# Mamba block with routed experts: the state's four output rows scaled on ScalarE and accumulated into y by DMA

## The reference

```
def step(s, inp):
    d_t, B_t, C_t, u_t = inp
    dA = jnp.exp(d_t[..., None] * A)
    dBu = d_t[..., None] * B_t[:, None, :] * u_t[..., None]
    s = s * dA + dBu
    y = jnp.einsum('bds,bs->bd', s, C_t)
    return (s, y)
...
y = y * jax.nn.silu(z)
```

## Time and profile before

| | us |
|---|---|
| median of 2 runs | 3052.15 |
| the profiled execution, as a run | 3054.61 |
| its span (first to last instruction) | 3052.8 |

### The profile page before, as it was taken

How to read it: one execution, slowest core, us unless ns; L and a number is a source line. 1 busy time by engine, 2 the same in 40 slices (tenths; PEclk the granted TensorE clock), 3 DMA queues, 4 the chain that set the end, 5 groups by cost and what they waited for, 6 DMA issues and landing times.

```text
span 3052.8 us, 52878 instructions
## 1 busy us (share of the span) xinstructions
PE 2488.1 (82%) x16524; PEld 1983.2 (65%) x16524; DVE 2568.1 (84%) x3986; ACT 1830.3 (60%) x3484; POOL 2563.1 (84%) x2379
## 2 busy tenths in 40 slices
PE   2566988879888797988879798887979888797979
PEld 0344766757676675767667576776757667576767
DVE  3579899888898988889898888889888898988953
ACT  2666666666666665665657566665656656665531
POOL 1689898989989898998989889898988989898942
PEclk7557998999999998999989899999989999999989
DMA  1311111211112111121112111121212211111101
GB/s 64 107 56 58 64 56 64 71 57 61 56 61 72 62 61 53 60 68 64 63 52 77 56 60 59 64 66 55 74 41 73 68 56 60 60 58 58 67 32 49
DMA packets 62150, 187.97 MB, mean 62 GB/s; under 512 B 12040, under 2 KB 14728, under 8 KB 61488
## 3 DMA queue, kind: packets, MB, share of 16 engines
q1 hardware_dynamic: 61872, 184.58, 18.0%
HBM read 166.68 MB, written 17.87 MB: 60 GB/s over the span
## 4 chain that ended last, share of the span: by engine, by line
POOL 29%; PE 27%; DVE 17%; issue 16%; ACT 9%; DVEq 1%; POOLq 1%; ACTq 0%; DMA 0%
POOL db_sb L639 12%; PE bank_ps L1236 9%; DVE states L995 7%; POOL y_sb L651 6%; PE moe_ps L1251 6%; PE rows_ps L1178 5%; POOL act L681 3%; POOL y_sb L659 2%; PE bank_ps L1160 2%; ACT da_ps L839 2%; DVE y_sb L1014 2%; DVE bank_ps L950 2%; DVE act L1089 1%; PE bank_ps L1134 1%; POOL du_sb L628 1%
## 5 line engine op out<-in xcount | busy, mean ns | idle before, releaser
L639 POOL TENSOR_TENSOR db_sb<-du_sb,b_sb 128x512 f32<-128x512 f32 x1024 | 1296.6, 1275 | 0.1
L1178 PE MATMUL rows_ps<-ident,states 128*128 128x128 f32 x4096 | 673.2, 295 | 163.7 <-DVE states L995 94.3
L651 POOL TENSOR_TENSOR y_sb<-y_sb,c_rows 128x512 f32<-128x512 f32 x512 | 655.1, 1280 | 169.8 <-ACT c_rows L817 169.8
L839 ACT ACTIVATE da_ps<-delta,a_sb 128x512 f32<-128x512 f32 x1024 | 701.8, 687 | 85.7 <-DVE states L995 84.2
L1178 PEld LDWEIGHTS rows_ps<-ident,states 128*128 128x128 f32 x4096 | 535.3, 153 | 281.9 <-DVE states L995 133.0
L1251 PE MATMUL moe_ps<-eout_sb,act 128*128 128x256 f32 x2304 | 627.7, 396 | 85.2 <-POOL act L681 83.5
L1236 PE MATMUL bank_ps<-h2T_high,ein_w_high 128*128 128x256 f16 x2304 | 644.0, 280 | 21.8 <-DVE delta L971 12.0
L995 DVE TENSOR_TENSOR_SCAN states<-da_ps,carry,db_sb 128x512 f32<-128x512 f32 x512 | 648.4, 1274 | 15.0 <-ACT da_ps L839 13.2
L1236 PE MATMUL bank_ps<-h2T_high,ein_w_low 128*128 128x256 f16 x2304 | 643.1, 279 | 0.0
L1236 PE MATMUL bank_ps<-h2T_low,ein_w_high 128*128 128x256 f16 x2304 | 642.4, 279 | 0.0
L995 DVE TENSOR_TENSOR_SCAN states<-da_ps,db_sb 128x512 f32<-128x512 f32 x512 | 616.2, 1213 | 23.2 <-ACT da_ps L839 13.0
(11 more groups left out here) (156 smaller groups left out, 2851.1 us busy)
## 6 DMA issues: line engine op xcount, KB each, us to landing
b_sb<-b_dram SPq DMA_DIRECT2D x128, 512.0 KB, 3.6
w_sb<-w_dram SPq DMA_DIRECT2D x128, 512.0 KB, 4.0
th_p<-x_dram SPq DMA_DIRECT2D x16, 512.0 KB, 5.8
r_dram<-conv SPq DMA_DIRECT2D x16, 512.0 KB, 2.6
x<-r_dram SPq DMA_DIRECT2D x16, 512.0 KB, 3.8
out_dram<-x SPq DMA_DIRECT2D x32, 256.0 KB, 2.2
mod_p<-mod_dram SPq DMA_DIRECT2D x8, 384.0 KB, 6.2
x<-e_in_dram SPq DMA_DIRECT2D x5, 512.0 KB, 4.6
```

The lines of the kernel that those rows point to most:

```text
L639: pool.tensor_tensor(db_sb[:, n % NDB, :], du_sb[:, slots[t][0][0], b, :], b_sb[:, k % NBPAIR, s % BPAIR, :], ALU.mult).then_inc(sem["scal ...
L651: pool.tensor_tensor(place, place, c_rows[:, n % NCR, :], ALU.add).then_inc(sem["c_added"], 1)
L839: ac.activation(da_ps[n % NDA][:, :], delta[:, slots[t][0][0], b, :], ACT.Exp, scale=a_sb[:, b, s:s + 1]).then_inc(sem["exp_done"], 1)
L1178: last = pe.transpose(rows_ps[j % 2][:, b * P:b * P + P], states[:, step % 2 * NB + b, j * P:j * P + P], ident[:, :])
```

## The change

All four groups of a state go the same way now. `c_scale` on ScalarE scales all four; two neighbouring groups (CPAIR = 2) go side by side into one buffer of c_rows, which has NCR = 3 buffers of 128x2x512. `c_add` no longer computes: for each pair GpSimd issues one accumulating DMA (512 KB) that adds c_rows to y_sb. It waits for the pair's second c_scale and for the same pair's transfer of the state before to have landed. `c_scale` waits for the transfer that last read its buffer. `y_gate` waits for the last transfer of its pair. `gather` is gone. To make room, db_sb has 5 buffers instead of 6 and w_sb holds 2 experts for each buffer instead of 4, so w_load runs twice as often with half the bytes. Some 20 due-time shifts change by fractions of a unit.

```
-NDA, NDB, NCR = 2, 6, 3
-C_ACT = (1, 3)
+NDA, NDB, NCR = 2, 5, 3
+CPAIR = 2
-WROWS, NWROWS = 4, 2
+WROWS, NWROWS = 2, 2
...
-            out += [(at + 0.145, ("c_scale", t, s, j)), (at + 0.892, ("c_add", t, s, j))] if j in C_ACT else [(at + 0.156, ("gather", t, s, j))]
+            out.append((at + 0.145, ("c_scale", t, s, j)))
+            if j % CPAIR == CPAIR - 1:
+                out.append((at + 0.892, ("c_add", t, s, j // CPAIR)))
...
-        c_rows = sb("c_rows", [P, NCR, DI])
+        c_rows = sb("c_rows", [P, NCR, CPAIR, DI])
...
+            def c_adds(n):
+                return sem[f"c_added{n % (NJ // CPAIR)}"], 16 * (n // (NJ // CPAIR) + 1)
...
-                    def c_add(t, s, j):
+                    def c_add(t, s, pair):
                         step = NS * nS(t) + s
-                        n = len(C_ACT) * step + C_ACT.index(j)
-                        pool.wait_ge(*c_scales(step, j))
-                        pool.wait_ge(sem["c_added"], max(0, n - len(C_ACT) + 1))
+                        n = NJ // CPAIR * step + pair
+                        pool.wait_ge(*c_scales(step, CPAIR * pair + CPAIR - 1))
+                        if step:
+                            pool.wait_ge(*c_adds(n - NJ // CPAIR))
...
-                        place = y_sb[:, slots[t][0][0], j, :]
-                        pool.tensor_tensor(place, place, c_rows[:, n % NCR, :], ALU.add).then_inc(sem["c_added"], 1)
+                        pool.dma_start(y_sb[:, slots[t][0][0], CPAIR * pair:CPAIR * pair + CPAIR, :], c_rows[:, n % NCR, :, :],
+                                       accum_op=ALU.add).then_inc(c_adds(n)[0], 16)
...
-                            pool.wait_ge(*((sem["c_added"], nS(t) * NS * len(C_ACT)) if j in C_ACT else (sem["gathered"], nS(t) * NS * len(C_DVE))))
+                            pool.wait_ge(*c_adds(NJ // CPAIR * (nS(t) * NS - 1) + j // CPAIR))
...
                     def c_scale(t, s, j):
...
-                        ac.wait_ge(sem["c_added"], max(0, n - NCR + 1))
-                        ac.activation(c_rows[:, n % NCR, :], rows_ps[j % 2][:, :], ACT.Copy,
+                        if n >= NCR:
+                            ac.wait_ge(*c_adds(n - NCR))
+                        ac.activation(c_rows[:, n % NCR, j % CPAIR, :], rows_ps[j % 2][:, :], ACT.Copy,
...
-                    def gather(t, s, j):
...
-                            pe.wait_ge(*(c_scales(*before) if before[1] in C_ACT else gathers(*before)))
+                            pe.wait_ge(*c_scales(*before))
```

More of the change, by code:

```diff
@@ L46 @@
 NPAIR = NE // 2 + 1
-NDA, NDB, NCR = 2, 6, 3
-C_ACT = (1, 3)
-C_DVE = tuple(j for j in range(NJ) if j not in C_ACT)
+NDA, NDB, NCR = 2, 5, 3
+CPAIR = 2
 NBANK = 3
@@ L140 @@
 TICK, ROUTED, UNITS_END = 1.4601, 16.0, 63.872
-SOFT = 45.462
+SOFT = 45.427
 Z_AHEAD, Y_SOON, Y_LATE = -0.26, -2.597, 0.993
 SLOT = 67.197
[L144 to L152, removed]
@@ new lines @@
+SHIFT = {"b_load": 0.39, "b_store": 0.49, "c_add": 0.79, "c_scale": 0.59, "delta": -0.77, "dt_bias": 0.09, "du": -0.32, "e_act": -0.12,
+         "e_mul": -0.12, "e_tanh": -0.35, "e_weigh": 0.65, "ein_load": 0.17, "ein_low": 0.44, "eout_fold": 0.63, "eout_load": -0.11,
+         "exp": 0.87, "expert_in": -0.12, "expert_out": 0.65, "gather": 0.59, "h2_high": 0.21, "h2_low": 1.04, "h_rms": -0.31,
+         "h_scale": -0.62, "h_square": -0.36, "hn_high": -0.93, "hn_low": -0.62, "hn_t": -0.65, "logit_exp": 0.21, "op": 0.69,
+         "op_gate": 0.69, "out_add": -0.12, "out_gate": -0.21, "out_store": 0.38, "r_add": 3.69, "r_gate": -0.15, "r_store": 0.35,
+         "router": 1.67, "rows": 0.41, "scaled": -0.1, "scan": -0.15, "skip": -1.61, "skip_evac": -0.34, "skip_t": -0.32, "soft_exp": -0.4,
+         "soft_ln": 0.93, "tap": 0.14, "u": -0.55, "u_tanh": -0.55, "w_evac": 0.99, "w_load": -0.12, "w_t": 0.94, "x1": 0.69,
+         "x1_norm": 0.93, "x1_rstd": -0.41, "x1_stat": 0.69, "x_load": -2.41, "x_rstd": -0.61, "x_scale": 0.42, "x_stat": 0.15,
+         "xd_t": -0.08, "xd_t_evac": 0.27, "y_evac": 0.39, "y_gate": -0.15, "y_t": 0.69, "z": -0.44, "z_gate": -0.51, "z_tanh": -0.45}
@@ L306, in adaln_block @@
                 "e_tanhed", "e_acted", "e_weighed", "expert_out_done", "out_gated", "out_added",
-                "exp_done", "scaled_done", "c_scaled", "c_added", "scan_done", "carried", "rows_full", "gathered",
+                "exp_done", "scaled_done", "c_scaled", "c_added0", "c_added1", "scan_done", "carried", "rows_full",
                 *(f"bank_{what}{n}" for what in ("full", "free") for n in range(NBANK)),
@@ L466, in h_done @@
                 return bank_read(("x_norm", t, half))
-            def gathers(step, j):
-                return sem["gathered"], len(C_DVE) * step + C_DVE.index(j) + 1
             def c_scales(step, j):
-                return sem["c_scaled"], len(C_ACT) * step + C_ACT.index(j) + 1
+                return sem["c_scaled"], NJ * step + j + 1
+            def c_adds(n):
+                return sem[f"c_added{n % (NJ // CPAIR)}"], 16 * (n // (NJ // CPAIR) + 1)
             def walk(steps):
@@ L813, in c_scale @@
                         step = NS * nS(t) + s
-                        n = len(C_ACT) * step + C_ACT.index(j)
+                        n = NJ // CPAIR * step + j // CPAIR
                         ac.wait_ge(sem["rows_full"], NJ * step + j + 1)
-                        ac.wait_ge(sem["c_added"], max(0, n - NCR + 1))
-                        ac.activation(c_rows[:, n % NCR, :], rows_ps[j % 2][:, :], ACT.Copy,
+                        if n >= NCR:
+                            ac.wait_ge(*c_adds(n - NCR))
+                        ac.activation(c_rows[:, n % NCR, j % CPAIR, :], rows_ps[j % 2][:, :], ACT.Copy,
                                       scale=xd_sb[:, slots[t][0][0], j, AT_C + s:AT_C + s + 1]).then_inc(sem["c_scaled"], 1)
@@ L1001, in carries @@
                         return sum(max(0, min(NS, step + 1 - NS * nS(t))) for t in halves)
-                    def gather(t, s, j):
-                        step = NS * nS(t) + s
-                        par = slots[t][0][0]
-                        v.wait_ge(sem["rows_full"], NJ * step + j + 1)
-                        if step:
-                            v.wait_ge(*gathers(step - 1, j))
-                        if s == 0 and t > 0 and slots[t - 1][1] is not None:
-                            v.wait_ge(*bank_read(("skip_t", t - 1, NB - 1)))
-                        place = y_sb[:, par, j, :]
-                        v.scalar_tensor_tensor(place, rows_ps[j % 2][:, :], xd_sb[:, par, j, AT_C + s:AT_C + s + 1], place,
-                                               ALU.mult, ALU.add).then_inc(sem["gathered"], 1)
                     def z_gate(t, j):
@@ L1115, in _ @@
                     walk({"ein_low": ein_low, "x_stat": x_stat, "x_scale": x_scale, "x_shift": x_shift, "tap": tap,
-                          "u": u, "xd_evac": xd_evac, "delta": delta_, "hn_low": hn_low, "h2_low": h2_low, "scan": scan, "gather": gather,
+                          "u": u, "xd_evac": xd_evac, "delta": delta_, "hn_low": hn_low, "h2_low": h2_low, "scan": scan,
                           "z_gate": z_gate, "op_gate": op_gate, "x1": x1_, "x1_stat": x1_stat, "router": router, "e_act": e_act, "e_mul": e_mul,
```

## The result

The changed kernel takes 3092.01 us, the median of two runs (3088.16 and 3095.86), against 3052.15 before: 1.28% slower, ratio 1.0128, 95% interval 1.0096 to 1.0160. That is within 2%, so the two kernels count as about equal; but the whole interval lies above 1, while 2930 us, a gain, was forecast.

What follows compares the result with a forecast made beforehand. GpSimd was taken as the bound: 120.5 us kept plus 33.3 of issues plus 18 idle make a slot of 171.8 us instead of 179.4. Over sixteen slots that is 122 us off 3052, so 2930 us, full range 2800 to 3250.

Steps and rivals of the forecast that it cites:

- The bound: Whole slot of 179.4 us: GpSimd, 160.0 us busy and 19.4 idle, sets the pace.
- The price of an issue: GpSimd's 32 DMA issues a slot: 1.04 us each, 33.3 us, bounded by 0.32 and 2.37 us.
- The idle time: GpSimd's waits in a slot: 18 us, of which c_rows 9, y_gate's landing 3, w_sb 2.5, expert product 1.5.
- the prediction's formula: Slot length as GpSimd's busy plus idle time: 138.5 + 32 p us, p the price of an issue, with 18 us idle.
- The landing: At the slot's turn, y_gate waits for the last transfer: lands after about 5.5 us, GpSimd stands 3 us.
- Costed at nothing: Five db_sb buffers, 128 more issues on SyncE's queue and three c_rows buffers: no time added.
- The wait at the head of ScalarE's list: ScalarE's c_scale waits delay exps and scans: taken as nothing, another 10 us a slot if VectorE's room were gone.
- Rival (a): GpSimd's issue is dear: slower from 1.40 us an issue, 3217 us at 1.6; 22 in 100.
- Rival (b): DMA engines become the bound: accumulating transfer at four times a copy's time, 6.2 us, gives 3868 us; 8 in 100.
- Rival (c): GpSimd's issue costs only 0.32 us, TensorE takes over: slot 165.4 us, time 2828 us; 12 in 100.
- Rival (d): Nothing to be seen, about 3040 us; sign: scans wait for exps 8 us a slot or more; 20 in 100.
- The inner range: Forecast's own range, 2850 to 3010 us: issue price from 0.8 to 1.16 us, idle time 3 us off either way.

Runs made afterwards that it cites:

- the kernel without additions: Kernel before the change with GpSimd's 512 additions of c_rows to y_sb left out, all else as it was: 2968.6 us, ratio 0.9718.
- the one with half the transfers: Kernel before with only GpSimd's additions (groups 1 and 3) replaced by one accumulating transfer a state: 3080.3 us; with the last state on GpSimd 3028.5 us.

## Why the prediction was wrong, point by point

- **The bound.** This step failed: "GpSimd is thus the main bound and the sum below goes by its time". Time freed on GpSimd arrives by 5.1 in 39.5, as the kernel without additions shows. In the middle GpSimd, TensorE and VectorE are all near full; at the turn nearly the whole price of the transfers is paid (11.8 of 12.7 us). Adding busy and idle time of one engine treats its idle time as a sum of waits that can be costed one by one, but idle time is where the other engines' pace shows.
- **The price of an issue.** 1.04 us was taken. Measured by GpSimd's busy time it is (149.9 - 120.5) / 32 = 0.92 us, 846 ns for one after idle. The busy-like time of 153.8 us was nearly right (149.9). But the additions were counted by the pitch, and by the pitch an issue is 0.61 us; the rest is lateness. That 1.04 us came near is luck: the row it was taken from is an operation on 4 elements. The Trainium skill ("DMA: Bandwidth & Descriptors", "Specifications") has about 1 us to a first byte on this path; no view here shows a first byte, and the smallest copy has landed 1.8 us after its issue began.
- **The idle time.** This is the term of the sum that was mis-sized: 18 us were forecast, 31.8 came: c_rows 14.6 instead of 9 (177.0 / 12.11), w_sb 3.4 instead of 2.5, delta 2.8 instead of 1, the same pair's earlier transfer 2.2 instead of 0, the norms' steps 3.2 where about 1 was taken for all short steps. It turned 7.6 us of gain into 2.3 of loss. By the prediction's formula with the measured 0.92 the slot would be 167.9 us; it is 181.7.
- **The landing.** Right in size: 5.8 us to land (about 5.5 forecast), 3.4 us of y_gate's wait (3 forecast). Wrong in weight: it was one term among GpSimd's waits, but TensorE stands behind it too, with the steps of the turn behind it. Keeping the last landing away from y_gate gave 30 us in the changed kernel and 52 in the one with half the transfers.
- **Costed at nothing.** The three c_rows buffers and the same pair's earlier transfer: ScalarE waits 20.9 / 12.11 = 1.7 us a slot for a buffer and GpSimd 2.2 for the pair. The wait at the head of ScalarE's list: "I take nothing", but c_scale behind a stand of 8.8 us holds TensorE and GpSimd in state 3.
- **Left out.** What 512 KB transfers at a DMA share of 0.69 do to others: x lands after 8.2 us instead of 5.8, and VectorE waits 2.8 us a slot for it.
- **The due-time shifts.** Not costed at all. They cost 31 us, where the loss against the kernel before is 40. They do not explain the miss: without them the kernel stands at 3060.8 us, not at 2930.
- **Rival (a)**, a dear issue: price below its threshold of 1.28, so not this. **Rival (b)**, the DMA engines as the bound: 2.80 us a transfer against a forecast of 3.1, a DMA share of 0.69 against some 0.74, so they fit, as was said. But an engine share under 1 was not free: 72 us come with the accumulation's size. The Trainium skill ("Collectives: The Full Stack", "The bandwidth ceiling") has a reduction among cores at half a copy's rate for its two source reads; the traces agree with the ratio, 2.15 times the copy's time, and show nothing of its cause. **Rival (c)**: not reached. **Rival (d)**, "nothing to be seen", was nearest, at 3040 us, and partly by the way it named, head-of-line waits on ScalarE. Its sign came short of its 8 us: scans waited 87.6 / 12.11 = 7.2 us a slot for exps, and VectorE had 40 us of idle time for that.
- The inner range of 2850 to 3010 us does not follow from its own terms. At p = 0.8 the formula gives 164.1 us, less than rival (c)'s floor of 165.4, so 2828; at p = 1.16 with 3 us more of idle time it gives 178.6, so 3039.
- The full range of 2800 to 3250 us held the time; direction and mechanism were wrong, and that the range held is luck.

## What to carry to other kernels

Before an engine's freed time is counted as gain, cut the period finely and look at every engine in each piece: where two or three are near full together, relief of one brought a small fraction here, and the cheap test is a kernel that leaves the work out. Ask also what the new transfers do to the landings of the old ones. A transfer that replaces an engine's work adds a landing to every chain that ends in it, so keep it off the last step ahead of a consumer and give it the operands that are consumed last. An order tuned by hand is a change of its own: try old and new order on both kernels. What db_sb's and w_sb's smaller buffers cost by themselves was not tried.

## What the runs showed of the hardware

- An accumulating 512 KB transfer within SBUF takes 2.80 us of all 16 DMA engines and lands in 5.8 us, at a DMA share of 0.69; the same transfer as a copy 1.30 and 3.3, at 0.46.
- Its issue occupies GpSimd for 846 ns with one piece a partition and 1186 with two; a copy's 591. The next instruction starts after 0.61 us all the same (0.77 with two pieces), and then ends late: by 0.31 us more after each issue in the stretch shown, and on time again once GpSimd has waited long enough. In the changed kernel `scaled` averages 1902 ns with an unchanged pitch of 1.24 us (1612.85 - 1611.61, the start of the next instruction). After a copy's issue nothing is late (1275 ns). The Trainium skill ("GPSIMD Engine Reference", "4. When to use GPSIMD") says that a pair of the engine's cores writes the descriptors; that the other cores run ahead and these two lag is my reading, which no run here shows.
- An accumulating transfer of 64 bytes a partition uses 144 packets, like one of 4 KB (73728 / 512), and a copy of the same 64 bytes 32 (16384 / 512). The queue of the two kernels, accumulating and copying:

```profile
q0 software_dynamic: 73728, 4.23, 4.3%
```

```profile
q0 software_dynamic: 16384, 4.23, 0.7%
```
